# Attention on one Trainium2 core: the value product in two wide steps per four heads, and a new order of the work around it

## What is computed

```
x = layernorm(x)
Q = rope(x @ wq); K = rope(ctx @ wk); V = ctx @ wv      # 16, 2, 2 heads of 32
scores = Q @ K.T / sqrt(32); scores = where(mask == 0, -1e9, scores)
out = softmax(scores) @ V; x2 = x + out @ wo
y = x2 + moe(layernorm(x2))                              # 8 experts, top 2, and a shared one
```

## Time and profile before

| | |
|---|---|
| median of three runs | 1559.9 us |
| profiled execution, its own time | 1558.8 us |
| its span, first to last instruction | 1557.0 us |
| TensorE busy | 1451.6 us, 93% |
| VectorE, ScalarE, GpSimd busy | 955.2, 910.6, 532.4 us |
| matmuls of the value product | 4096, busy 139.6 us |
| attention phase | to about 862 us |

### The profile page before, as it was taken

One profiled execution on the slowest core, in us unless ns is written; L12 is line 12 of the kernel. 1 busy time (PEld: TensorE's weight loads), 2 busy tenths in 40 slices (PEclk: granted clock), 3 DMA queues, 4 the chain that ended last, 5 costly groups with the idle time before them and its releaser, 6 DMA issues. The chain is left out here.

```text
span 1557.0 us, 37250 instructions
## 1 busy us (share of the span) xinstructions
PE 1451.6 (93%) x11434; PEld 1179.1 (76%) x11434; DVE 955.2 (61%) x2635; ACT 910.6 (58%) x2050; POOL 532.4 (34%) x665
## 2 busy tenths in 40 slices
PE   4699999999999989999989489999999999999997
PEld 3487787887887868878767367888888888888885
DVE  4487777867778778687766366666565333333332
ACT  2389888887889878888897232222221344444442
POOL 2133232331432314223222143222224455546553
PEclk9799999999999999999999789999999999999999
DMA  4234345444354443544434513222225877886652
GB/s 153 68 110 127 110 122 160 124 133 125 110 163 124 137 130 113 154 120 131 129 99 145 190 64 82 82 89 81 91 80 168 238 194 178 203 232 118 111 89 35
DMA packets 141482, 198.94 MB, mean 128 GB/s; under 512 B 34903, under 2 KB 72543, under 8 KB 141282
## 3 DMA queue, kind: packets, MB, share of 16 engines
q1 hardware_dynamic: 120738, 157.81, 33.3%
q0 software_dynamic: 17952, 33.64, 11.6%
q10 hardware_dynamic: 2592, 4.98, 0.9%
HBM read 97.10 MB, written 69.35 MB: 107 GB/s over the span
## 5 line engine op out<-in xcount | busy, mean ns | idle before, releaser
L896 DVE CUSTOM_DVE_ANT_0 a_probs<-a_psum,a_bias 128x512 f32<-128x512 f32 x512 | 348.6, 686 | 168.4 <-PE a_psum L711 156.8
L528 ACT ACTIVATE a_probs<-a_probs,a_low 128x512 f32<-128x512 f32 x512 | 369.0, 721 | 105.4 <-DVE a_low L896 101.2
L623 PE MATMUL a_psum<-a_ident,a_probs 128*128 128x128 f32 x2048 | 318.2, 278 | 19.3 <-DVE a_xT_lo L843 6.2
L623 PEld LDWEIGHTS a_psum<-a_ident,a_probs 128*128 128x128 f32 x2048 | 242.7, 141 | 90.7 <-issue 38.3
L711 PE MATMUL a_psum<-a_kT,a_q_stack 128*128 128x512 f32 x512 | 249.5, 488 | 9.1 <-DMA a_q_stack<-a_qT_lo 5.6
L534 ACT ACTIVATE a_probsT<-a_psum 128x512 f32<-128x512 f32 x400 | 234.2, 586 | 12.1 <-issue 6.6
L1246 POOL DMA_INDIRECT out<-b_y,b_pairs_sb x71 | 113.2, 1594 | 147.2 <-DMA out<-b_y,b_pairs_sb 87.2
L730 PE MATMUL a_psum<-a_probsT,a_v 128*32 128x128 f32 x4096 | 139.6, 277 | 7.4 <-ACT a_probsT L534 4.7
L1689 DVE SCALAR_TENSOR_TENSOR b_v_hidden<-b_v_hidden,b_psum 128x256 f32<-128x256 f32 x71 | 29.9, 421 | 165.3 <-ACT b_v_hidden L1348 165.3
L730 PEld LDWEIGHTS a_psum<-a_probsT,a_v 128*32 128x32 f32 x4096 | 105.1, 110 | 30.0 <-issue 17.4
L446 POOL CAST a_w_hi<-a_w_raw 128x256 fp32r<-128x256 f32 x96 | 38.6, 402 | 259.4 <-DMA a_w_raw<-in_L_ffn_Wd 126.3
(11 more groups left out here) (206 smaller groups left out, 3156.6 us busy)
## 6 DMA issues: line engine op xcount, KB each, us to landing
b_w<-w_halves SPq DMA_DIRECT2D x16, 1536.0 KB
a_q_stack<-a_qT_hi SPq DMA_DIRECT2D x256, 64.0 KB, 2.0
a_q_stack<-a_qT_lo SPq DMA_DIRECT2D x256, 64.0 KB, 2.0
w_halves<-a_w_hi SPq DMA_DIRECT2D x96, 128.0 KB, 1.8
w_halves<-a_w_lo SPq DMA_DIRECT2D x96, 128.0 KB, 1.9
a_x_in<-in_x SPq DMA_DIRECT2D x32, 256.0 KB, 2.9
a_ctx_in<-in_ctx SPq DMA_DIRECT2D x32, 256.0 KB, 3.9
a_x_res<-in_x SPq DMA_DIRECT2D x32, 256.0 KB, 3.0
```

Of the source, the lines that this page charges most:

```text
L528: nc.scalar.activation(probs[:, h % 2, t], probs[:, h % 2, t], ACT.Exp, bias=low[:, h % H, t:t + 1], scale=-1.0, accum_out=total[:, h // G ...
L623: last = nc.tensor.transpose(out[:, P * i:P * (i + 1)], src(i), identity[:])
L896: nc.vector.tensor_tensor_reduce(probs[:, h % 2, t], psum[:, t % 2], bias[:, t], 1.0, HUGE, ALU.add, ALU.min, low[:, h % H, t:t + 1]).then ...
```

## The change

The value product of a group is made in two steps of two query tiles each. A matmul streams 256 columns, from two slots of probsT (`turned` gives the slots). The buffer probsT has three doubled slots instead of four. The steps stand behind unit 15 (tiles 0 and 1) and unit 22 (tiles 2 and 3) of the group, and each waits for copies that are two units or more back. All other work beside the units stands in three tables by unit, one each for TensorE, ScalarE (by half units) and VectorE; GpSimd's three tables change by a head here and there. SP's order stays. VectorE copies 20 tiles of 64 instead of 14. The order of one unit stays: transposes, scores six ahead, other work.

```diff
-DOUBLED = (0, 1, 1, 2)
-DVE_EVACUATES = ((3,), (1,), (), (3,), (3,), (), (), (3,), (1,), (3,), (), (1,), (1, 3), (3,), (1, 3), (3,))
+AHEAD = 6
+DOUBLED = (0, 0, 2, 1)
+OUT_STEPS = ((0, 2, 3), (2, 2, 10))
+DVE_EVACUATES = ((), (0,), (1, 2), (1,), (0,), (0, 3), (), (2,), (0, 2), (1, 3), (), (0,), (1, 2), (0,), (1, 3), (2, 3))
+PE_AT = {
+    0: (('inverse', -1),), 1: (('ctxT', 0),), 4: (('xT', 0),), 5: (('spread', -1),), 6: (('out', -1),), 8: (('q', 0),), 9: (('q', 1),),
+    11: (('q', 2),), 12: (('q', 3),), 13: (('xT', 1),), 15: (('qT', 2), ('out', 0)), 16: (('q', 4), ('q', 5), ('inverse', 0)), 17: (('kv', 0),),
+    18: (('ctxT', 1),), 19: (('q', 6), ('q', 7)), 21: (('spread', 0), ('xT', 2)), 22: (('out', 0),), 24: (('q', 8),), 25: (('kT', 0),),
+    26: (('qT', 3), ('q', 9)), 27: (('kv', 1), ('q', 10)), 28: (('ctxT', 2),), 29: (('q', 11), ('xT', 3)), 31: (('out', 1),),
...
+    40: (('wo', 0), ('wo', 1)), 42: (('kT', 1),), 43: (('wo', 2), ('wo', 3)), 44: (('qT', 4), ('ctxT', 3)), 45: (('wo', 4), ('wo', 5)),
...
+    52: (('kT', 3), ('wo', 10)), 53: (('wo', 11), ('spread', 2)), 54: (('out', 2),), 55: (('wo', 12),), 57: (('wo', 13),), 59: (('wo', 14),),
+    61: (('qT', 5),), 62: (('wo', 15),), 63: (('out', 3),),
+}
+ACT_AT = {
...
+    32: (('inverse', 0),), 36: (('ctxT', 1),), 42: (('xT', 2),), 43: (('spread', 0),), 50: (('att_hi', 0),), 52: (('qT', 3),), 57: (('ctxT', 2),),
...
+    107: (('spread', 2),), 114: (('att_hi', 2),), 123: (('qT', 5),),
+}
+DVE_AT = {
+    0: (('stats', 0),), 1: (('moments', 0),), 2: (('xn', 0),), 5: (('x_low', 0),), 6: (('stats', 1), ('moments', 1)), 7: (('att', -1),),
+    11: (('xn', 1),), 13: (('q', 0),), 14: (('x_low', 1),), 15: (('inverse', 0),), 16: (('q_low', 2), ('stats', 2)), 17: (('kv', 0),),
...
+    27: (('q_low', 3), ('kv', 1)), 28: (('xn', 3),), 29: (('q', 2),), 30: (('x_low', 3),), 31: (('inverse', 1),), 34: (('kv', 2),), 38: (('q', 3),),
...
+}
...
-        K_HEADS = {4: 0, 7: 1, 10: 2, 12: 3}
+        X_HEADS = {0: 0, 1: 1, 4: 2, 6: 3}
+        Q_HEADS = {3: 0, 5: 1, 7: 2, 9: 3}
+        K_HEADS = {4: 0, 6: 1, 8: 2, 11: 3}
+        LOW_HEAD = 2
...
+        def turned(h, t, tiles, c):
+
+            at = [ring(h, i) for i in range(t, t + tiles)]
+            step = at[1] - at[0] if tiles > 1 else 1
+            if all(b - a == step for a, b in zip(at, at[1:])):
+                return probsT[:, at[0]:at[-1] + 1:step, P * c:P * (c + 1)]
...
-                def weighted(b, par, g, t):
-
-                    n = TT * (GH * g + GH - 1) + t + 1
+                def weighted(b, par, g, t, tiles):
+
+                    n = TT * (GH * g + GH - 1) + t + tiles
...
-                            last = nc.tensor.matmul(psum[DK * j:DK * (j + 1), OUT, P * t:P * (t + 1)], v[:, batch, c, DK * (h // REP):DK * (h // REP + 1)],
-                                                    probsT[:, ring(h, t), P * c:P * (c + 1)], start=(c == 0), stop=(c == TT - 1))
-                    if t == TT - 1:
+                            last = nc.tensor.matmul(psum[DK * j:DK * (j + 1), OUT, P * t:P * (t + tiles)], v[:, batch, c, DK * (h // REP):DK * (h // REP + 1)],
+                                                    turned(h, t, tiles, c), start=(c == 0), stop=(c == TT - 1))
+                    if t + tiles == TT:
...
+                    for u in range(H * TT):
+                        turn_probs(part, b, u // TT, u % TT)
+                        if u + AHEAD < H * TT or part != "last":
+                            scores(b, par, (u + AHEAD) // TT, u % TT ^ 2)
+                        beside(part, b, par, u)
```

More of the change, by code:

```diff
@@ L135, in attention_phase @@
         stacked = [ctx.enter_context(nc.semaphore(f"a_stacked{i}")) for i in range(GH)]
[L137 to L141, removed]
@@ L166, in products_at, with there @@
[L166 to L169, removed]
-            if part != "first":
-                out += [("wo", t, at.index((h, pos))) for t, at in enumerate(WO_AT) if (h, pos) in at]
-            return out
-        def weighted_at(part, h):
-            g, t = (h // GH, 0) if h % GH == GH - 1 else (h // GH - 1, h % GH + 1)
-            return None if part == "first" and g < 0 else (g, t)
+        def there(part, kind, i):
+            if kind in ("inverse", "spread", "out", "att", "att_hi"):
+                return part in ("middle", "last") or part == "first" and i >= 0 or part == "end" and i < 0 and kind != "out"
+            if kind in ("qT", "q_low"):
+                return part in ("first", "middle") or part == "last" and i < HG
+            if kind in ("wo", "add"):
+                return part in ("middle", "last")
+            if kind == "probs":
+                return part in ("first", "middle", "last")
+            return part in ("first", "middle")
@@ L179, in group_done, with stages @@
+        def stages(part, table, at):
+            return [(kind, i) for kind, i in table.get(at, ()) if there(part, kind, i)]
         def group_done(part, h):
@@ L182, in group_done @@
             return None if part == "first" and g < 0 else g
-        def turns(part):
-            return [turn_at(part, h, pos) for h in range(H) for pos in range(4) if turn_at(part, h, pos)]
         start = [("xT", 0), ("ctxT", 0)]
@@ L193, in attention_phase @@
         start += [("qT", HG), ("qT", HG + 1)]
-        orders = {"start": start, "first": turns("first"), "middle": turns("middle"), "last": turns("last"),
-                  "end": [("inverse", -1), ("spread", -1)]}
         before = {"middle": "middle", "last": "middle", "end": "last"}
@@ L220, in t_bank @@
             return ring_bank("middle", "probs", TT * h + t)
-        def there(part, kind, i):
-            return part != "end" if kind == "probs" else (kind, i) in orders[part]
         def in_bank_before(part, at):
@@ L758, in beside @@
                             spread_inverse(part, b, i)
-                    if pos == 1 and weighted_at(part, h):
-                        weighted(b, par, *weighted_at(part, h))
-                    products()
+                        if kind == "out":
+                            for t, tiles, after in OUT_STEPS:
+                                if (GH * i + GH - 1) * TT + after == u:
+                                    weighted(b, par, i, t, tiles)
+                        if kind == "q":
+                            project_q(part, b, i // DC, i % DC)
+                        if kind == "wo":
+                            project_out(part, b, par, i // DC, i % DC)
                 def body(part, b, par):
@@ L784, in body @@
                         turn_inverse(part, b, -1)
-                        weighted(b, par, -1, 1)
-                        weighted(b, par, -1, 2)
+                        for t, tiles, after in OUT_STEPS:
+                            if TT * (GH * HG - 1) + after >= H * TT:
+                                weighted(b, par, -1, t, tiles)
                         spread_inverse(part, b, -1)
-                        weighted(b, par, -1, 3)
                         for t in range(TT):
```

205 lines of the change are left out of this document (72 added, 133 removed), and 2 rows, old and new, of the table PE_AT.

## The result

The changed kernel takes 1584.5 us in the median (1582.2 to 1584.8, four runs), the kernel before, run beside it, 1560.5: a ratio of 1.0148, 95% interval 1.013 to 1.0165. It is slower by 24 us; 1547 was forecast. The profiled execution took 1584.8 us, with a span of 1583.0.

What follows compares the result with a forecast made beforehand. TensorE's order of work was taken to bound the kernel (busy 93% of the span). Terms -12.8, -18.0 and +18.5 sum to -12.3 us, giving 1547 us, range 1527 to 1571.

Steps and rivals of the forecast that it cites:

- part 3: Earlier query transposes wait for the previous group's copies into q_stack: +18.5 us, between 3 and 56.
- group 3: Transposes moved from unit 31 to 26; TensorE loses 1.5 us per batch in unit 28, 12.0 us in all.
- part 1: Value product: half as many steps, twice as wide, save 64 x 0.19 us of whole-to-quarter-array passages: -12.8 us.
- part 2: TensorE waits removed by the new order, 12.0 us in middle batches, rest in first and last: -18.0 us.
- Group 4: Transposes moved from unit 47 to 44, waiting for the previous group's copies: 0.2 x 8 = 1.6 us lost.
- Group 5: Transposes moved from unit 63 to 61, copies late near the batch's end: 0.7 x 7 = 4.9 us lost.
- The slower side: Rival: copies into q_stack land as late as in the earlier trace, costing 45 us: 1574 us, chance 0.26.
- the wide step saves nothing: Rival: a wide set of the value product costs as much as 0.25 us: 1560 us, chance 0.12.
- weight loads pace the step: Rival: 2048 fewer weight loads in the value product save 52.6 us more: 1495 us, chance 0.02.
- Middle batches outside 98 to 101 us: Sign: a middle batch not between 98 and 101 us would show the prediction wrong.
- ScalarE's wait of 3 to 4 us: Sign: ScalarE waits this long for q_stack in unit 26, TensorE 1 to 2 us before unit 28's context transposes.
- Over 5 us: Sign: if ScalarE waits over 5 us for q_stack in unit 26, the slower case holds.

Runs made afterwards that it cites:

- sp_first: Changed kernel with SP issuing the last four q_stack copies of groups 2 to 4 ahead of a weight piece, which follows one head later: 1572.4 us, ratio 1.0061.
- old_two_buffers2: Kernel before, order and narrow steps kept, with two qT_hi and two qT_lo buffers in turn, two small buffers given up for room: 1555.6 us, ratio 0.9974.
- q_two_buffers: Changed kernel, order untouched, with two qT_hi and two qT_lo buffers used in turn: 1535.3 us, ratio 0.9844; on another occasion 1534.1 us, 0.9834.
- tb_narrow: Changed kernel with two qT_hi and qT_lo buffers and four one-tile value steps per group, two of them one unit earlier: 1555.0 us, ratio 0.9951.
- q3_late: Changed kernel with query group 3's transposes, ScalarE copy and VectorE low half moved back, the transposes from unit 26 to 31: 1551.5 us, ratio 0.9937.
- tb_narrow_pairs: Changed kernel with two qT_hi and qT_lo buffers, each wide step replaced by two one-tile steps back to back: 1535.3 us, ratio 0.9841.

## Why the prediction was wrong

**The failed step is the price of part 3,** 1.5 us for group 3, which rested on a landing 5.4 us behind the score. The shape of that step was right: the loss is the landing less 3.9. The landing was 7.0 in the row above and 4.9 to 8.6 over the batches, 6.9 on the average, because SP still issued a weight piece ahead of the copies (with SP free, in sp_first, it was 4.4 to 6.2 in the first seven batches). I had let the earlier split of the piece free the queue, and chosen a value between two rows where the earlier trace rows showed the late one. By the landing signals in the trace of the kernel before, the last of the same copies landed 5.5 to 8.2 us behind the score of unit 25 in the first seven batches, 7.4 on the average, and 13.5 us behind it in the last: 5.4 lay under every batch. By the same formula 7.0 gives 3.1 us, and 3.08 is the wait in the row. The 1.4 us of half pace behind it were in no term. Together that is 4.5 us a batch; 4.9 was measured.

By its terms, in us:

| term | forecast | measured | from |
|---|---|---|---|
| part 1, passages | -12.8 | -9.3 | work, before to changed |
| part 2, waits removed | -18.0 | -12 | waiting, old_two_buffers2 to the two runs of q_two_buffers (-14.0, -9.7) |
| part 3, copies | +18.5 | +44 | waiting, changed less those two (+49), less the 5.1 that the copies cost before |
| sum | -12.3 | +23 | first to last score: +22.5 |

**Part 1.** The wide set costs 0.219 us, as forecast (0.21 to 0.23), a step lies 1.87 us ahead of the next work (1.9), no cost of the read from two slots is seen. A pair of steps cost 2.21 with its passages, a wide one costs 1.96: 0.25 a pair, 16 us for 64. Only 9.3 arrived. A part is seen in the starts: 32 of the old steps stood right behind the spread matmul, and the next start comes 0.42 behind that one whether a step follows or a transpose. These 32 passages (0.09 each, 2.9 us) were never separate. The remaining 4 us are as much as the new order adds to the work when the steps stay narrow (719.2 before, 723.1 in tb_narrow); which of its places cost them, no run shows. "64 x 0.19" counted every step as if it stood behind a score.

**Part 2.** The x transposes in unit 4 wait for nothing, as forecast, and the middle batches get their 12 us or a little more (outside the edges and the units above, waiting falls from 20.2 to 6.8). The last batch, given 3.5, and the first, given 2.0, show nothing: 10.7 and 12.8 us in old_two_buffers2, 10.7 and 13.7 in q_two_buffers. The value steps of the last batch no longer wait, but other work does in their place. The six more VectorE copies, priced at nothing, are probably worth 6 to 7 us, and are in the -12.

**Part 3.** Group 3: 12 forecast, about 36 us more than before measured. Group 4: 1.6 forecast, 9 measured; and q3_late shows that it would be more without the stall ahead of it. Group 5: 4.9 forecast, nothing clear at the edges (14.6 to 16.4). The upper bound of 56 is 55 by its own terms (29.6, 17.5 and 8).

**The rivals.** The slower side was the right one: the place, the queue and the point of decision (a landing from 6.6 us) held. Its price for the copies was 45 us, near the 44 measured, but that is partly luck: it had 26, 13 and 6 us for groups 3, 5 and 4, where some 36, nothing clear and 9 came. Its 3.2 us for group 3 is also less than its own formula gives for the landing of the earlier trace rows (7.6 less 3.9 is 3.7), and it had nothing for the clock. Its 1574 came out too low since it kept the full 30.8 of gains, where 21 came. It had a chance of 0.26, and the range ended at 1571, inside its own case. That the wide step saves nothing is refuted by its sets of 0.219 us, where 0.25 was needed, and by the 20 us between tb_narrow and q_two_buffers; that weight loads pace the step is refuted by tb_narrow_pairs.

**The signs named.** Middle batches outside 98 to 101 us were to show the prediction wrong, and they did (103.2 on the average). ScalarE's wait of 3 to 4 us was right (3.29), TensorE's of 1 to 2 was not (3.08). "Over 5 us" as the mark of the slower case was wrong: ScalarE comes to the copy only at 416.41, 2.2 us behind the transposes, so its wait is as long as TensorE's, not longer.

## What to carry to other kernels

Before a step is moved up, follow what it waits for back to the queue that serves it, and price the landing by the row that shows this queue at work, not by a value between busy and free. A wait is cheaper to remove than to place: another position in the order moved it to the next group, another one in the queue to the batch edges, and 4 KB per partition of second buffers ended it. And a passage counts only where its neighbours do not make one anyway.

## What the hardware showed that was not expected

A standstill of 3.1 us left TensorE at a granted clock of 0.50, which is 1.2 GHz, for some 3 us behind it (421.08 to near 424), which made 1.89 us of work 3.29; with 13 idle matmuls in its place it stayed at 1.00. The Trainium skill, page "TensorE: Matmul & The Clock Gate", part 1, says that an idle TensorE falls to 1.2 GHz and comes back once it has been busy; the trace agrees. It could have been read ahead: in the earlier trace rows the four transposes behind a wait of 2.94 us last 1.09, and 0.60 elsewhere, while the steps behind waits of 1.4 us in the earlier trace rows keep their 1.08. Also, 32 fp32 products on four column groups with 128 columns, and half as many with 256, take the same time within 0.02 us, weight loads included. And copies that were issued alike did not land alike: in sp_first the fourth was issued 2.3 us behind the score in each of the first seven batches, and landed 4.4 to 6.2 us behind it.
